# Weighted one-hot rows of a graph layer: two wide VectorE operations replaced by eight narrow ones that read PSUM

## The reference, cut to what matters

```
C   = 0.5 * (cos(edge_weight * PI / 10) + 1) * (0 <= edge_weight <= 10)
h   = gelu(edge_attr @ f_w0 + f_b0)          # 50 -> 128
h   = gelu(h @ f_w1 + f_b1); h = gelu(h @ f_w2 + f_b2); h = gelu(h @ f_w3 + f_b3)
xf  = x @ lin1_w
msg = xf[src] * (h * C[:, None])
agg = segment_sum(msg, dst, num_segments=1250)
out = gelu(agg @ lin2_w + lin2_b) @ lin_w + lin_b
x   = layernorm(x + out)
```

## Time and profile before

| | |
|---|---|
| median of 3 runs | 243.63 us (242.91 to 243.84) |
| the profiled execution: its time / its span | 242.63 us / 240.8 us |
| TensorE busy | 219.4 us, 91% |
| GpSimd busy | 177.1 us, 74%, of which gathers L303 166.8 us |
| VectorE busy | 146.0 us, 61% |
| ScalarE busy | 111.6 us, 46% |

### The profile page before, as it was taken

One profiled execution on the slowest core, in us unless ns is written; L12 is line 12 of the kernel. 1 busy time (PEld: TensorE's weight loads), 2 busy tenths in 40 slices (PEclk: granted clock), 3 DMA queues, 4 the chain that ended last, 5 costly groups with the idle time before them and its releaser, 6 DMA issues.

```text
span 240.8 us, 4025 instructions
## 1 busy us (share of the span) xinstructions
PE 219.4 (91%) x1182; PEld 146.6 (61%) x1182; DVE 146.0 (61%) x271; ACT 111.6 (46%) x185; POOL 177.1 (74%) x151
## 2 busy tenths in 40 slices
PE   2799799999999999999999999999999999984670
PEld 3546466767567675676756767667676676783350
DVE  6697157566666666656666566665666656683144
ACT  2763754652644526445264452644526455210053
POOL 6777777887777777787777777878777777786000
PEclk9999999999999999999999999999999999998577
DMA  6842131322212222122221222212122121111003
GB/s 225 241 127 65 51 79 43 78 59 62 73 45 77 60 57 77 43 75 52 68 72 43 72 57 62 77 45 75 43 72 76 40 76 43 46 36 45 5 0 108
DMA packets 17440, 16.55 MB, mean 69 GB/s; under 512 B 8988, under 2 KB 14907, under 8 KB 17429
## 3 DMA queue, kind: packets, MB, share of 16 engines
q0 software_dynamic: 10976, 9.26, 16.1%
q1 hardware_dynamic: 5728, 6.58, 9.0%
q10 hardware_dynamic: 726, 0.60, 0.8%
HBM read 15.00 MB, written 1.28 MB: 68 GB/s over the span
## 4 chain that ended last, share of the span: by engine, by line
POOL 56%; issue 17%; PE 11%; DVE 6%; ACT 3%; DMA 3%; POOLq 1%; DVEq 1%; SPq 0%; ACTq 0%
POOL gathered L303 56%; DMA gathered<-xf_dram,src_idx 1%; DMA lin_xT_sb<-in_lin_xT 1%; PE ps_even L602 1%; ACT h L333 1%; PE ps_even L475 1%; PE ps_even L453 1%; PE ps_even L438 1%; PE ps_agg L502 1%; PE ps_pick L533 1%; PE ps_odd L475 1%; PE ps_odd L602 1%; PE ps_odd L438 1%; POOLq L60 1%; PE ps_odd L462 1%
## 5 line engine op out<-in xcount | busy, mean ns | idle before, releaser
L303 POOL DMA_INDIRECT gathered<-xf_dram,src_idx x134 | 166.8, 1245 | 40.9 <-issue 40.9
L333 ACT ACTIVATE h<-ps_odd,biases_sb 128x500 f32<-128x500 f32 x61 | 41.3, 677 | 25.1 <-PE ps_odd L467 19.0
L333 ACT ACTIVATE h<-ps_even,biases_sb 128x500 f32<-128x500 f32 x61 | 40.8, 669 | 24.3 <-PE ps_even L467 22.6
L331 ACT ACTIVATE h<-pre 125x512 f32<-125x512 f32 x40 | 25.0, 625 | 50.9 <-DVE pre L706 50.9
L502 PEld LDWEIGHTS ps_agg<-onehot,messages 125*128 125x128 f32 x304 | 38.3, 191 | 10.4 <-issue 9.2
L502 PE MATMUL ps_agg<-onehot,messages 125*128 125x64 f32 x304 | 40.0, 274 | 0.8 <-DVE messages L722 0.8
L766 DVE TENSOR_TENSOR pick<-ps_pick,node_ids 128x1250 bf16<-128x1250 f32 x18 | 26.3, 1459 | 23.8 <-PE ps_pick L526 23.8
L533 PE MATMUL ps_pick<-xf_parts,pick 128*125 128x384 bf16 x180 | 33.1, 331 | 0.0
L533 PEld LDWEIGHTS ps_pick<-xf_parts,pick 128*125 128x125 bf16 x180 | 23.1, 136 | 16.3 <-issue 12.5
L722 DVE TENSOR_TENSOR messages<-h,gathered 125x512 f32<-125x512 f32 x37 | 25.4, 688 | 5.6 <-DVE gathered L741 3.4
L475 PEld LDWEIGHTS ps_odd<-w_mlp_sb,h 128*125 128x125 f32 x160 | 20.5, 188 | 8.7 <-issue 8.7
(11 more groups left out here) (126 smaller groups left out, 189.3 us busy)
## 6 DMA issues: line engine op xcount, KB each, us to landing
edge_in<-in_edge_attrT SPq DMA_DIRECT2D x44, 97.7 KB
gathered<-xf_dram,src_idx POOLq DMA_INDIRECT x134, 3.3
xf_dram<-xf_sb SPq DMA_DIRECT2D x2, 256.0 KB
lin_xT_sb<-in_lin_xT SPq DMA_DIRECT2D x1, 369.0 KB, 4.1
lin_xT_sb<-in_lin_xT SPq DMA_DIRECT2D x1, 320.0 KB, 2.9
w_mlp_sb<-in_w_mlp ACTq DMA_DIRECT2D x1, 256.0 KB
out<-normed SPq DMA_DIRECT2D x1, 256.0 KB
out<-normed SPq DMA_DIRECT2D x1, 192.0 KB
```

The costliest lines, as they stand in the source:

```text
L303: nc.gpsimd.indirect_dma_start(out=gathered[0:TILE, b, t, :], out_offset=None, in_=xf_dram[:, :], in_offset=bass.IndirectOffsetOnAxis(ap=s ...
L331: nc.scalar.activation(out_ap, in_ap, GELU).then_inc(done, 1)
L333: nc.scalar.activation(out_ap, in_ap, GELU, bias=biases_sb[:, layer:layer + 1]).then_inc(done, 1)
```

## The change

The eight tiles of a pair get one operation each in place of the two wide ones. `tensor_scalar` on 125 x 64 elements compares the node columns with a per-partition value `dst_rel[:, tile]` and multiplies by a per-partition value `cut[:, tile]`. The node columns are a copy in PSUM, columns 128 to 191 of bank `ps_agg`, made once a pass after the first raw message has been read out of that bank. `hit` and its semaphore go.

For pair 0, the order on VectorE changes: first raw message, copy of the columns, eight one-hot operations, second raw message. The message semaphore that lets the scatter of group 0 start is now set by the eighth one-hot operation. In the last turn, the one-hots of pairs 18 and 19 are made before the last two `add_bias4`. In all other pairs they stay in their place.

```diff
--- before.py
+++ after.py
@@ -111,7 +111,6 @@
         pre4 = sb("pre4", [TILE, 4, TILES_PER_GROUP, FEAT])
         h4 = sb("h4", [TILE, 4, TILES_PER_GROUP, FEAT])
         messages = sb("messages", [TILE, 4, TILES_PER_GROUP, FEAT])
-        hit = sb("hit", [TILE, PAIR_TILES, WINDOW])
         onehot = sb("onehot", [TILE, 2, PAIR_TILES, WINDOW])
         aggT = sb("aggT", [FEAT, AGG_COLS])
 
@@ -146,6 +145,7 @@
         xf_bank = (ps4[0], ps4[1], ps_pick)
         pieces = ((0, 2), (2, 6), (6, NODE_CHUNKS))
         node_bank = (ps1[0], ps1[1], ps23[0])
+        columns_bank = ps_agg[0:TILE, 2 * WINDOW:3 * WINDOW]
         last_agg = (ps23[0][:, 0:WINDOW], ps1[0][:, 0:WINDOW])
         halves = ((0, 2, ps23[1]), (2, 6, ps4[0]), (6, 8, ps4[1]), (8, NODE_CHUNKS, ps_pick))
 
@@ -201,13 +201,15 @@
         act3_done = sem("act3_done")
         act4_done = sem("act4_done")
         bias4_done = sem("bias4_done")
-        hit_done = sem("hit_done")
         message_done = sem("message_done")
         group_begun = sem("group_begun")
         scatter_done = sem("scatter_done")
         agg_added = sem("agg_added")
         last_landed = [sem(f"last_landed_{t}") for t in range(TILES_PER_GROUP)]
         last_message = sem("last_message")
+        columns_copied = sem("columns_copied")
+        copies_begun = sem("copies_begun")
+        raw_used = sem("raw_used")
         gather_landed = [sem(f"gather_landed_{s}") for s in range(GATHER_SLOTS)]
         x_biased = sem("x_biased")
         node2_done = sem("node2_done")
@@ -698,8 +700,7 @@
             passes = dve.value_load(passes_i[0:1, 0:1], min_val=1, max_val=MAX_PASSES)
             dve.wait_ge(w_loaded, 48)
             with dve.Fori(0, passes) as r:
-                nodes = iota_f[0:TILE, bass.ds(r * WINDOW, WINDOW)].rearrange("p (o n) -> p o n", o=1)\
-                    .to_broadcast((TILE, PAIR_TILES, WINDOW))
+                nodes = iota_f[0:TILE, bass.ds(r * WINDOW, WINDOW)]
 
                 def add_bias4(before, p, b):
                     dve.wait_ge(l4_done, before * (2 * TURN_PAIRS) + (2 * p + b + 1))
@@ -708,23 +709,28 @@
                         row_b3_sb[:, :].rearrange("p (o f) -> p o f", o=1).to_broadcast((TILE, TILES_PER_GROUP, FEAT)),
                         ALU.add).then_inc(bias4_done, 1)
 
-                def weigh_onehot(before, turn, p):
-                    tiles = bass.ds(turn * (TURN_PAIRS * PAIR_TILES) + p * PAIR_TILES, PAIR_TILES)
-                    dst = dst_rel[:, tiles].rearrange("p (t o) -> p t o", o=1).to_broadcast((TILE, PAIR_TILES, WINDOW))
-                    factor = cut[:, tiles].rearrange("p (t o) -> p t o", o=1).to_broadcast((TILE, PAIR_TILES, WINDOW))
-                    nc.vector.tensor_tensor(hit[:, :, :], dst, nodes, ALU.is_equal).then_inc(hit_done, 1)
-                    dve.wait_ge(hit_done, before * TURN_PAIRS + (p + 1))
-                    nc.vector.tensor_tensor(onehot[:, p % 2, :, :], hit[:, :, :], factor, ALU.mult)
+                def weigh_onehot(turn, p):
+                    first_tile = turn * (TURN_PAIRS * PAIR_TILES) + p * PAIR_TILES
+                    for t in range(PAIR_TILES):
+                        tile = bass.ds(first_tile + t, 1)
+                        ins = nc.vector.tensor_scalar(onehot[:, p % 2, t, :], columns_bank, dst_rel[:, tile], cut[:, tile],
+                                                      ALU.is_equal, ALU.mult)
+                    return ins
 
                 def message(before, p, b, rows_of_x):
                     dve.wait_ge(act4_done, before * (2 * TURN_PAIRS) + (2 * p + b + 1))
                     slot = (2 * p + b) % 4
-                    nc.vector.tensor_tensor(messages[:, slot, :, :], h4[:, slot, :, :], rows_of_x, ALU.mult)\
-                        .then_inc(message_done, 1)
+                    return nc.vector.tensor_tensor(messages[:, slot, :, :], h4[:, slot, :, :], rows_of_x, ALU.mult)
 
                 def message_raw(g):
                     dve.wait_ge(raw_product, r * RAW_GROUPS + g + 1)
-                    message(first, 0, g, ps_raw[g][0:TILE, :].rearrange("p (t f) -> p t f", f=FEAT))
+                    return message(first, 0, g, ps_raw[g][0:TILE, :].rearrange("p (t f) -> p t f", f=FEAT))
+
+                def columns_to_psum():
+                    dve.wait_ge(raw_used, r + 1)
+                    dve.sem_inc(copies_begun, 1)
+                    nc.vector.tensor_copy(columns_bank, nodes).then_inc(columns_copied, 1)
+                    dve.wait_ge(columns_copied, r + 1)
 
                 def landed(slot, turn, p, per_use, per_pass):
                     dve.wait_ge(gather_landed[slot], r * (per_use * per_pass) + turn * per_use + per_use * uses_through(p))
@@ -732,7 +738,7 @@
                 def message_even(before, turn, p):
                     slot = 2 * p % GATHER_SLOTS
                     landed(slot, turn, p, 64, TURNS - (p % TURN_PAIRS == 0))
-                    message(before, p, 0, gathered[0:TILE, slot, :, :])
+                    message(before, p, 0, gathered[0:TILE, slot, :, :]).then_inc(message_done, 1)
 
                 def message_odd(before, turn, p):
                     slot = (2 * p + 1) % GATHER_SLOTS
@@ -744,7 +750,7 @@
                         axis=AX_X, op=ALU.add).then_inc(pick_summed, 1)
                     dve.wait_ge(pick_summed, number)
                     landed(slot, turn, p, 48, TURNS - (p % TURN_PAIRS in (0, TURN_PAIRS - 1)))
-                    message(before, p, 1, gathered[0:TILE, slot, :, :])
+                    message(before, p, 1, gathered[0:TILE, slot, :, :]).then_inc(message_done, 1)
 
                 def message_last(before):
                     for t in range(TILES_PER_GROUP):
@@ -777,11 +783,13 @@
                 def pair(before, turn, p):
                     add_bias4(before, p - 1, 0)
                     add_bias4(before, p - 1, 1)
-                    weigh_onehot(before, turn, p - 2)
                     if p == 2:
-                        message_raw(0)
-                        message_raw(1)
+                        message_raw(0).then_inc(raw_used, 1)
+                        columns_to_psum()
+                        weigh_onehot(turn, 0).then_inc(message_done, 1)
+                        message_raw(1).then_inc(message_done, 1)
                     else:
+                        weigh_onehot(turn, p - 2)
                         message_even(before, turn, p - 2)
                         message_odd(before, turn, p - 2)
                     build_pick(turn, p - 1)
@@ -799,12 +807,12 @@
                     for p in (4, 5, 6, 7):
                         pair(r * TURNS + j, j, p)
                 last = r * TURNS + LAST_TURN
+                weigh_onehot(LAST_TURN, 2)
+                weigh_onehot(LAST_TURN, 3)
                 add_bias4(last, 3, 0)
                 add_bias4(last, 3, 1)
-                weigh_onehot(last, LAST_TURN, 2)
                 message_even(last, LAST_TURN, 2)
                 message_odd(last, LAST_TURN, 2)
-                weigh_onehot(last, LAST_TURN, 3)
                 message_even(last, LAST_TURN, 3)
                 add_windows(last, 2)
                 message_last(last)
```

## The result

The changed kernel takes 247.22 us (median of four runs, 245.84 to 249.53), the kernel before 243.27 us beside it (242.61 to 243.84): a ratio of 1.0144, 95% interval 1.0087 to 1.0202. It is slower, and it lies outside the predicted range of 240.8 to 245.6. The profiled execution took 247.56 us, 4.93 more than that of before.

A forecast was written before the change was run, and what follows sets the result against it. GpSimd's unbroken gathers were taken to bound the kernel, with the compute stream close beside. A 1.1 us gain, stream losses hidden, made 242.63 - 1.1 = 241.5 us profiled, 242.5 against the median; range 240.8 to 245.6.

The forecast's parts named there:

- Cost of a new operation: VectorE: narrow one-hots 0.25 us from start to start, so a pair's one-hots take 2.0 us in place of 1.41.
- Steady state, cost nothing: Loop: longer one-hots fit before TensorE's scatter while their pitch stays under 0.316 us; pair period still 10.05 us.
- Rival (b): Loop: VectorE late for the scatter in each pair if one-hot pitch passes 0.316 us; slower, 245.4 at 0.33; chance 0.16.
- GpSimd's gain: Gathers: 5.6 us of excess by `hit` and `onehot` goes, messages then cost 6.2; last gather about 1.1 us sooner.
- Rival (c): Loop: one-hots reading PSUM hold up gathers all the same; 0 to +1.5 us, 243.6 to 245.1; chance 0.10.
- Pair 0, +1.75 us on the compute stream, once: Group 0's scatter waits for eight one-hots, matmuls start at 36.35; all later pairs 1.75 us later, GpSimd unaffected.
- The tail: Last turn: first bias at 215.5, TensorE's chain ends about 223.1; any gain capped at 2.1 us.
- A loss in the stream under about 2 us is hidden: Compute stream catches up and waits 1.98 us for a gather at pair 19, so smaller losses there do not show.
- 0.8 of 0.24 and a third of 0.50: Chance of faster by over 0.5%, given as 0.37: 0.8 of the well-falling-phases rival (0.24), a third of the forecast (0.50).
- The gather's rule: A gather starting inside a VectorE operation with two SBUF inputs gains excess: that operation's end less (start + 0.13).

The follow-up runs named there:

- e2_tail: Changed kernel with the tail in its old order (biases, eight narrow one-hots, messages, pair 19 by two wide operations); front as changed: 242.9 us, ratio 0.9949.
- e5_tailfill: Changed kernel plus four 128x500 matmuls that nobody reads in TensorE's idle stretch ahead of pair 18's scatter: 241.96 us, ratio 0.9898.
- e1_front: Changed kernel with pair 0's one-hots made by the two wide operations ahead of the first raw message; tail as changed: 243.31 us, ratio 1.0006.
- e4_filler: Changed kernel plus two 128x500 matmuls that nobody reads on TensorE just ahead of group 0's scatter: 246.82 us, ratio 1.0161.
- e9_front_tailfill: Changed kernel with pair 0's one-hots wide before the first raw message, plus four unread matmuls ahead of pair 18's scatter: 240.26 us, ratio 0.9867.
- e7_before_warm: Kernel before the change, plus extra unread matmuls in TensorE's idle stretches of the tail: 241.46 us, ratio 0.9927.
- e8_sbuf_cols: Changed kernel with wide one-hots for pairs 0 and 19, and narrow ones of pairs 1 to 18 reading node columns from SBUF: 243.25 us, ratio 0.9972.

## Why the prediction was wrong

- *Cost of a new operation*: right. 0.25 us was taken and 0.25 measured.
- *Steady state, cost nothing*: right. 10.06 us per pair. Rival (b) did not happen.
- *GpSimd's gain*: the mechanism was right (free one-hots, messages that catch the gathers released), and so was its size inside the loop. `hit`, `onehot` and messages cost 6.5 us of excess before; now messages cost 5.5 (17 gathers, predicted 6.2) and the 30 gathers that start under narrow one-hots 0.02, so 1.0 us is gained (forecast 1.1). It did not arrive: in this execution the prologue took 0.65 more (its cast 1.13 for 0.75, two other operations 0.27), and the first gather began 1.01 later. The last one starts at 220.70 for 220.35. Rival (c) fell.
- *Pair 0, +1.75 us on the compute stream, once*: the wait was priced rightly. It was 1.68, the matmuls came 1.84 late from the first raw message (36.58 - 33.21 for 34.60 - 33.07), and 1.94 is what e2_tail paid in all. But the step took TensorE's speed behind the wait as given. In the profiled execution the clock fell to 0.50 for about 6.8 us, and that cost another 3.24. It need not happen: the same wait in e2_tail and e5_tailfill left the clock at 1.00.
- *The tail*: this is the step that failed, here and in the two other traces with the changed tail and no filler in it (e1_front, e4_filler). It counted what VectorE does until the bias (predicted 215.5; measured 219.22: the sixteen one-hots took 4.12, as priced, but began at 215.17) and then moved TensorE's chain as a block to about 223.1, "and stays inside that"; it ended at 231.19 (227.68 + 3.51). The prediction never put down that TensorE is idle for 3.4 us there, nor what the clock does behind it: 10.19 us from pair 18's scatter to the last update, where e9_front_tailfill, with the clock at 1.00 and no wait for tiles, needs 226.42 - 220.61 = 5.81. That is 4.4 us.
- *"A loss in the stream under about 2 us is hidden"*: borne out by e2_tail, which lost 1.98 us by the end of the loop and still waited for its last gather. The loss in the changed kernel was not under 2 us.
- One sum is off by a hundredth: 0.8 of 0.24 and a third of 0.50 make 0.36 for faster, not 0.37. Nothing hangs on it.

The sum then reads: the stream reaches the tail 214.96 - 209.62 = 5.3 us late (predicted 1.75), and there it finds the chain 4.4 longer than at full clock. Three parts pass the gathers together: the wait at the front, the tail's order with its longer idle gap, and the half clock of the tail. With a full clock at the front all three together still take 246.82 us (e4_filler), and taking out any one of them is enough: the wait (e1_front, 243.31), the order (e2_tail, 242.9), the half clock (e5_tailfill, 241.96). So the fall of the clock at the front is not needed for the loss. How much it adds to the median of 247.22 is open: only one execution of the changed kernel has a trace, its mean clock is 0.951, and the other three have 0.953, which is also what e4_filler's profiled execution has, without that fall.

The Trainium skill (TensorE: Matmul & The Clock Gate, HAM oscillation — how this bites in real kernels) warns that waits between bursts of matmuls send the array back to its half clock, and that the next burst pays. The trace agrees in the tail: 3.43 us of idle time, then 0.50 from 222 us on. The prediction weighed two rules of the Trainium skill and not this one, which spoke against the change.

What stays open: what decides whether the clock falls. Behind the front's wait it fell in one profiled execution and not in two others. In the tail it fell behind 3.43 us of idle time and behind 1.52 (e2_tail); before, with 0.79 and then waits for single tiles, it fell at 221 us. Only the runs with fillers in the tail kept it. The three that kept it at the front with narrow one-hots there (e2_tail, e4_filler, e5_tailfill) had each had a fall at 12 to 16 us, in the prologue, and the changed kernel's had not. No run separates cause from coincidence.

## What to carry to other kernels

Price an idle gap of TensorE twice: its own length, and the work behind it at half clock, which may come or not. Then set the sum of all losses against the slack, not each loss by itself: here any two of the three could be hidden, and not all three. A gap in the last stage was the dear one here, since no stage follows in which to hide it; a few matmuls into a bank that nobody reads filled it (four of them: -5.3 us against the changed kernel). Fillers pay in the old kernel too (e7_before_warm, ratio 0.9927), so the times with fillers are no argument for narrow one-hots. And where two engines collide by phase, freeing one source of collisions tends to hand them to the next: count the excess that is left, not the excess removed.

## What the runs showed of the hardware

- The gather's rule held within 0.03 us through the loop of every trace, with one exception: the excess is the end of the message less (start of the gather + 0.13) (118.96: 119.37 - 118.96 - 0.13 = 0.28, and it took 1.48). The exception is a gather that starts 0.07 us ahead of a message and pays for it all the same (e9_front_tailfill at 87.43 took 1.83; e4_filler at 45.51, in pair 1, took 1.80). In the prologue other operations hold it up too: a long integer cast that starts up to 0.6 us behind the gather (e5_tailfill, 22.54: 2.20), and one with an input in PSUM (changed kernel, 18.23: 1.41). Narrow `tensor_scalar` operations with columns in SBUF and two per-partition values do not (e8_sbuf_cols).
- From SBUF the narrow operation is longer and follows sooner: 364 ns and eight in 1.87 us, against 334 ns and 2.10 us from PSUM.
- The same idle gap does not always have the same effect on the clock (1.68 us: 0.50 for about 6.8 us in one execution, 1.00 in two), so one profile is not enough to price it; the mean clocks of all runs tell more.
- A busy TensorE can stay at the lower level for long: in the changed kernel it is busy for all of 222 to 230 us, and the clock is 0.50 throughout.
